# Edge stage of a two-layer graph network: ScalarE fetches its rows behind the group's Silus

## What is computed

```python
h = jnp.maximum(_layernorm(x), 0.0)
x = x + gcn(h)                                   # layer 0: two graph convolutions
h = jnp.maximum(_layernorm(x), 0.0)
w = silu(edge_attr_64 @ We1 + be1) @ We2 + be2   # a row of 128 weights for each edge
m = w * (h[src] @ Wlin)                          # message: weights times a row by src
agg = segment_sum(m, dst, num_segments=6250)
x = x + h + silu(agg @ Wn1 + bn1) @ Wn2 + bn2
```

## Time and profile before

| | us |
|---|---|
| median of 3 runs | 4598.01 |
| lowest and highest run | 4581.12, 4602.13 |
| span of the profiled execution | 4560.4 |
| busy: PE, PEld, DVE, ACT, POOL | 3218.9, 2311.2, 2109.1, 949.7, 1449.0 |
| edge stage (1578 to 4505): busy PE, DVE, ACT, POOL | 1759.7, 781.5, 374.7, 1395.9 |

### The profile page before, as it was taken

The page is one execution under the profiler, slowest core; times in us unless marked ns, Lnnn a source line. Parts: engine busy times, 40 slices in busy tenths (PEclk is TensorE's granted clock), DMA queues, the critical chain, the costliest instruction groups (busy, mean ns, idle before and its releaser), DMA issues.

```text
span 4560.4 us, 82895 instructions
## 1 busy us (share of the span) xinstructions
PE 3218.9 (71%) x19882; PEld 2311.2 (51%) x19883; DVE 2109.1 (46%) x4806; ACT 949.7 (21%) x2058; POOL 1449.0 (32%) x1549
## 2 busy tenths in 40 slices
PE   6979999999889566555666555566566565565657
PEld 5624677777689444444444444444444344443445
DVE  8999999999844322222222222222222222222223
ACT  4112345555411111111111111111111111111111
POOL 0000000000000454444554445454445454444442
PEclk8989999999999676766777667667667777767667
DMA  1001122222379221222222212222122222222112
GB/s 47 0 0 43 57 86 86 114 113 102 157 293 348 73 53 46 54 50 51 54 53 53 49 45 56 49 55 49 47 49 55 50 53 52 55 51 53 48 49 56
DMA packets 289446, 325.50 MB, mean 71 GB/s; under 512 B 236303, under 2 KB 249640, under 8 KB 276606
## 3 DMA queue, kind: packets, MB, share of 16 engines
q1 hardware_dynamic: 234382, 218.90, 14.6%
q0 software_dynamic: 49504, 102.66, 8.7%
q10 hardware_dynamic: 5264, 1.36, 0.1%
HBM read 237.69 MB, written 85.09 MB: 71 GB/s over the span
## 4 chain that ended last, share of the span: by engine, by line
SPq 42%; PE 28%; issue 24%; DVE 3%; another core or an unknown queue 1%; DVEq 1%; ACT 0%; DMA 0%; POOL 0%; ACTq 0%; POOLq 0%
SPq L390 29%; SPq L386 10%; PE pb L1395 7%; PE pa L1395 7%; PE pc L1389 4%; PE pd L1389 4%; SPq L473 2%; PE pd L1353 2%; PE pf L1355 1%; PE pb L1480 1%; DVE shared L1030 1%; DVE loop L1030 0%; PE pa L1473 0%; DVEq L1030 0%
## 5 line engine op out<-in xcount | busy, mean ns | idle before, releaser
L544 POOL DMA_INDIRECT shared<-lin_table,idx x1516 | 1434.1, 946 | 1552.3 <-DVE shared L1204 657.3
L1554 PE MATMUL pb<-we_sb,shared 128*128 128x128 f32 x3136 | 704.6, 391 | 531.2 <-ACT shared L796 416.3
L1554 PEld LDWEIGHTS pb<-we_sb,shared 128*128 128x128 f32 x3136 | 596.5, 282 | 655.2 <-ACT shared L796 461.3
L796 ACT ACTIVATE shared<-pa,be_col 128x512 f32<-128x512 f32 x392 | 257.3, 685 | 2499.1 <-issue 2093.2
L1208 DVE TENSOR_TENSOR shared<-pb,shared 128x512 f32<-128x512 f32 x345 | 236.7, 689 | 958.9 <-DMA table_sb<-lin_table 660.8
L1550 PE MATMUL pb<-be_parts,ones 3*128 3x512 bf16 x392 | 189.6, 484 | 485.5 <-DVE shared L1208 484.3
L573 POOL DMA_DIRECT2D lin_table<-c x12 | 9.3, 772 | 1498.0 <-issue 1308.2
L1543 PE MATMUL pa<-shared,we_sb 64*128 64x512 f32 x784 | 393.0, 977 | 99.3 <-issue 94.9
L1225 DVE TENSOR_TENSOR agg<-agg,pf 128x128 f32 x98 | 28.3, 289 | 879.8 <-remote 817.9
L1030 DVE TENSOR_SCALAR shared<-col_h,shared 128x784 bf16<-128x784 f16 x1092 | 404.7, 420 | 5.0 <-issue 4.3
L1550 PEld LDWEIGHTS pb<-be_parts,ones 3*128 3x128 bf16 x392 | 36.9, 94 | 549.9 <-issue 524.1
(11 more groups left out here) (238 smaller groups left out, 4014.5 us busy)
## 6 DMA issues: line engine op xcount, KB each, us to landing
adjacency<-shared SPq DMA_DIRECT2D x49, 1568.0 KB, 5.6
shared<-adjacency SPq DMA_DIRECT2D x49, 1568.0 KB, 8.7
table_sb<-lin_table SPq DMA_DIRECT2D x3384, 0.5 KB
shared<-in_edge_attr_dram SPq DMA_DIRECT2D x195, 256.0 KB
table_sb<-lin_table ACTq DMA_DIRECT2D x2632, 0.5 KB
shared<-lin_table,idx POOLq DMA_INDIRECT x1516
lin_table<-c POOLq DMA_DIRECT2D x12, 256.0 KB, 7.3
out_dram<-xr SPq DMA_DIRECT2D x12, 256.0 KB
```

What stands on the lines that cost most here:

```text
L544: pool.indirect_dma_start(out=dest(s, j), out_offset=None, in_=table, in_offset=bass.IndirectOffsetOnAxis(ap=idx[:, s, j:j + 1], axis=0)). ...
L796: act.activation(act_t[:, h, :], pa[:, h, :], ACT.Silu, bias=be1_col[:, :]).then_inc(hid_act, 1)
L1554: last = pe.matmul(pb[:, h, i * F:(i + 1) * F], act_t[:, h, i * P:(i + 1) * P], we2_sb[:, :], start=False, stop=(i == 3))
```

## The change

In `edge_act`, the chunk of rows (the wait for `aside` in the first chunk of a turn, the load of the offsets, the 14 issues) moves from between the feature copy and the first Silu to behind the second Silu. Nothing else is changed.

```diff
                 act.activation(ea_t[:, :], pd[:, :], ACT.Copy).then_inc(ea_out, 1)
+                for h in range(2):
+                    act.wait_ge(hid_mm, g * 2 + (h + 1))
+                    if not isinstance(g, int) or g > 0:
+                        act.wait_ge(w_mm, g * 2 + (h - 1))
+                    act.activation(act_t[:, h, :], pa[:, h, :], ACT.Silu, bias=be1_col[:, :]).then_inc(hid_act, 1)
                 if rows is not None:
                     if rows[2] == 0 and not isinstance(rows[0], int):
                         act.wait_ge(msg_ready, (rows[0] - 1) * (2 * RING))
                         act.sem_inc(passed, 1)
                     fetch_rows(act, act_list, rows[0], rows[1], rows[2], SP_ROWS, ACT_ROWS // RING, act_rows_in)
-                for h in range(2):
-                    act.wait_ge(hid_mm, g * 2 + (h + 1))
-                    if not isinstance(g, int) or g > 0:
-                        act.wait_ge(w_mm, g * 2 + (h - 1))
-                    act.activation(act_t[:, h, :], pa[:, h, :], ACT.Silu, bias=be1_col[:, :]).then_inc(hid_act, 1)
```

## The result

The changed kernel takes 4197.95 us (median, 4190.64 to 4200.8), beside 4589.57 us (4560.17 to 4602.13) for the kernel before on the same chip: a ratio of 0.915, with a 95% interval of 0.9117 to 0.9183. (In all that follows, times are medians of all executions, and ratios leave out the few that fell in a slower state of the chip.) In the profiled executions the span fell from 4560.4 to 4188.9 us, by 371.5. All of it lies in the edge stage: the gathers begin at 1521 us in both and end at 4137 in place of 4505.

The account below looks back on a forecast made before the run. SP's queue of row transfers was taken as the bound at 61.9 us a turn; ScalarE at 58.5 and SP at 58.8 gave 58.5, saving 3.4 us in 46.75 turns, 161 us: 4598 - 161 = 4437 us, range 4350 to 4650.

Parts of the forecast that it names:

- What bounds the kernel: Edge stage: SP's queue, issuing 72 row transfers a turn without rest, sets the turn of 61.9 us.
- Step (1): ScalarE's Silus no longer stand behind 4.6 to 9.5 us of issues; by itself worth nothing.
- Step (2): Feature copy now behind ScalarE's 14 issues, so TensorE's first layer, 2.08 us, is no longer hidden: the price.
- Step (3): ScalarE's issues meet the gathers' stall in every group; ScalarE's cycle comes to 58.5 us a turn.
- the window: Stall of SP's and ScalarE's rows, supposed from 4.1 to 11.7 us after a burst of GpSimd's gathers begins.
- Step (4): GpSimd's bursts no longer join, the merged stall of 19 us goes, and SP's turn becomes 58.8 us.
- the short turn: Profiled turn of the old kernel, 3908.99 to 3967.81, 58.8 us, SP's rows 42.7; taken as SP's new turn.
- No change: Rival: stalls only move and SP pays the same, turn within 0.5 us of 61.9, 4575 to 4621 us; chance 0.13.
- Slower: Rival: evenly spaced stalls hit all four SP chunks, 12.2 us each, 4650 to 4730 us; chance 0.14.
- larger gain: Rival: ScalarE's 56.5 holds and stalls fall on SP's loads, turn near 55.5, 4300 us; chance 0.10.

Follow-up runs that it names:

- x_spst_before: Old order, SP's rows from fixed addresses (no load of offsets, no register moves), against the kernel before: 4197 us, ratio 0.937.
- x_few_after: New order, GpSimd gathering one tile a group in place of eight, against the kernel before: 3530 us, ratio 0.758.
- x_delay: Old order, each ScalarE chunk of rows first waiting for the first half of the first layer, against the kernel before: 4497 us, ratio 0.985.
- x_sems: New order with one useless semaphore increment ahead of each ScalarE row from a chunk's second on, against the kernel before: 4436 us, ratio 0.954.
- x_rest_before: Old order, GpSimd clearing an unread buffer four times behind each burst of gathers, against the kernel before: 4293 us, ratio 0.959.
- x_few_before: Old order, GpSimd gathering one tile a group in place of eight, against the kernel before: 3386 us, ratio 0.727.
- x_static: New order, ScalarE's rows from fixed addresses (no load of offsets, no register moves), against the kernel before: 4677 us, ratio 1.004.
- x_s0: Only ScalarE's chunk in the first of four groups moved behind the Silus, against the kernel before: 4736 us, ratio 1.038.
- x_rest2: Old order, GpSimd clearing an unread buffer twice behind each burst of gathers, against the kernel before: 4316 us, ratio 0.963.

## Why the forecast was right in direction and wrong in size

**What bounds the kernel** (SP's 72 rows, in chunks that meet the gathers' stall) was right. x_spst_before shows it: with SP relieved, the old order makes 4197 us at a ratio of 0.937. One row was misread on the way: the gather at 3377.18 is the eighth of its own burst, not the first of the next. That one comes 1.25 us later, at 3378.42, and just as closely behind, so the argument stands.

**Step (1)**, the Silus are worth nothing by themselves: holds. x_few_after, where they are early and no stall is left to avoid, is the slower one. Two Silus follow the feature copy at 2.8 us (3009.66 to 3012.49), as said.

**Step (2)**, the price of the first layer: the mechanism is right, and the x_few pair puts it at 3.3 us a turn or more. The cycle without the rows is a little dearer than I had it: from four index copies in the turn (3006.90 to 3060.59, 53.7 us) take ScalarE's rows (5.88, 7.22, 8.37 and 6.87, together 28.3) and 25.4 us are left, where I had 58.5 less 36.7, 21.8.

**Step (3)** failed, and with it the size. I took the window as fixed, 4.1 to 11.7 us after a burst's begin, and had every chunk of ScalarE cross it: 9.2 to 9.6 us a chunk, 36.7 a turn. Measured are 28.3, 8.4 less. With the 3.6 more from step (2) this is 58.5 - 8.4 + 3.6 = 53.7 us. The stall is no fixed stretch after the burst's begin: it opened at 3.2 us before and at 7.3 after (medians), and its end stayed, 1.8 us behind the last gather. What sets the opening stays open. The two queues had issued 11 rows since the burst's begin when it opened before the change and 14 after it (medians), which looks like a stock that is used up, reached later because ScalarE's rows now stand behind the Silus. But the same count gives 10 in x_delay, where 64 of 180 bursts have no such row at all, and 8 in x_sems, so no one number of rows fits.

**Step (4)** was right in its mechanism and too small, and it failed by the same window. In the loop no two bursts are 0.3 us apart, the chunks of 19 to 22 us are gone (two, of 18 and 20 us, are left behind it, at the end of the stage), and x_rest_before shows that this by itself, with nothing of ScalarE moved, is worth 4.1%. But the short turn (58.8 us) that I took for the new one was no picture of even bursts: its rests are 3.6 us at one place and 9.2 at another. SP's chunks came to 32 us in the turn shown, where I carried over 42.7; SP has time left, and ScalarE is the bound. Since the longer of the two queues sets the turn, either of the two costs that were too high, 36.7 for ScalarE's rows or 42.7 for SP's, would have held the forecast up by itself. That both queues stood at 58.5 to 58.8 was chance.

**The rivals.** "No change" would have needed prices of rows that hold wherever they stand; x_few_before and x_static refute that. "Slower" (four chunks of 12.2) didn't come about in the changed kernel. x_s0 is 3.8% slower than before, but through bursts run together, not through evenly bad ones. The "larger gain" had the right direction and a tenth of the chance; even its 4300 was too high.

## What to carry to other kernels

Where an engine's instructions are dear only beside another engine's bursts of transfers, look first at the rests between the bursts: an engine that gets quicker can lose all of its gain by starting the next burst too early, and useless work on the engine that bursts shows how much of the loss, at least, is pace. Here that was 4.1% where the change gained 8.5%; then look where in a burst the dear instructions stand. A part of such a change says little on the whole: here one moved chunk of four costs 3.8%, three gain 7.6%, four gain 8.5% (each against its own runs of before).

## What the runs showed of the hardware

- While GpSimd issues a run of indirect gathers (one per 1.25 us), SP and ScalarE each come into a state in which an instruction takes about 0.70 us, a register move or a semaphore increment as well as a transfer, where an undisturbed row (move and transfer) is 0.32. It opened 3.2 us (before) or 7.3 us (after) behind the first gather's begin in the median, and ended 1.8 us behind the last one's end. With single gathers SP has 20 of 3196 row spacings over 0.55 us, against 1165 before. One engine can be in it while the other isn't (x_static).
- Of two bursts that run together, SP's chunk in the second is slow throughout: 19 to 22 us for 18 rows in 23 chunks of the kernel before. A rest of 1.8 us of enforced work (x_rest2, 3.5 in the median in fact) is enough to end this: no chunk there is over 14.4 us.
- Two queues beside each other issue rows at the price of one, 0.32 us (x_few_before).
- A load of offsets to registers takes 1.4 and 3.2 us by turns where its 56 bytes begin at 0 and 8 mod 16, 1.56 and 3.85 for 72 bytes, and 0.96 and 1.37 for 48 and 80 bytes, which never begin at 8 (medians). The Trainium skill (DMA: Bandwidth & Descriptors, section "Latency and other measured facts") has a floor of about 600 ns for such a load; the quickest median here, 0.96 us, is above it, and a begin at 8 adds 1.8 to 2.3 us.
- TensorE's granted clock is 0.789 in the mean before, 0.829 after and 0.892 in x_few_after: it was higher the shorter the turn was (0.770 in x_s0). No run tells how much of the time a higher clock gave. TensorE isn't what the edge stage waits for in the earlier trace rows; after the change its first layer is 8% of the chain, so some of it may hang on the clock.
